# A conditioned transformer layer on one core: the front's stacks built and loaded by halves of the heads, the weight preparation moved, and one output projection placed among the score blocks

## What is computed

```python
c6 = jax.nn.silu(c) @ Wc + bc
sh_msa, sc_msa, g_msa, sh_mlp, sc_mlp, g_mlp = jnp.split(c6, 6, axis=-1)
xm = _modulate(_ln(x), sh_msa, sc_msa)
q, k, v = (xm @ Wq + bq), (xm @ Wk + bk), (xm @ Wv + bv)   # 16 heads of 16 features
w = softmax((q / DH) @ k^T)                                # 512 x 512 for each head
x = x + g_msa[:, None, :] * ((w @ v) @ Wo + bo)
xm2 = _modulate(_ln(x), sh_mlp, sc_mlp)
h = jax.nn.gelu(xm2 @ W1 + b1, approximate=False)          # 1024 wide
x = x + g_mlp[:, None, :] * (h @ W2 + b2)
```

## Time and profile before

| | us |
|---|---|
| median of three runs | 772.96 |
| the three runs | 769.92, 773.67, 772.96 |
| the profiled execution | 769.82 |
| its span in the profile | 768.0 |

### The profile page before, as it was taken

One profiled execution on the slowest core, in us unless ns is written; L12 is line 12 of the kernel. 1 busy time (PEld: TensorE's weight loads), 2 busy tenths in 40 slices (PEclk: granted clock), 3 DMA queues, 4 the chain that ended last, 5 costly groups with the idle time before them and its releaser, 6 DMA issues.

```text
span 768.0 us, 10579 instructions
## 1 busy us (share of the span) xinstructions
PE 709.2 (92%) x3967; PEld 383.4 (50%) x3967; DVE 580.4 (76%) x1019; ACT 391.3 (51%) x463; POOL 216.8 (28%) x162
## 2 busy tenths in 40 slices
PE   4698989869999999999999999999999998998986
PEld 2451222432368425762378326852477226812976
DVE  4779788859886998789887988789887976621463
ACT  5420556117752675358642875267633773398221
POOL 1454020200344032512253033413062122230444
PEclk8875799869999999999999999999999998999999
DMA  8599000771058302850067303930175102021110
GB/s 299 204 260 254 22 29 15 254 175 55 29 174 228 99 29 100 248 165 29 28 213 176 111 28 125 257 117 29 45 259 142 55 29 72 15 71 45 56 35 28
DMA packets 59839, 88.36 MB, mean 115 GB/s; under 512 B 6246, under 2 KB 47740, under 8 KB 56716
## 3 DMA queue, kind: packets, MB, share of 16 engines
q1 hardware_dynamic: 59788, 87.69, 37.4%
HBM read 49.35 MB, written 38.06 MB: 114 GB/s over the span
## 4 chain that ended last, share of the span: by engine, by line
PE 67%; DVE 16%; issue 6%; DMA 5%; ACT 4%; POOL 1%; SPq 0%; ACTq 0%; DVEq 0%
PE ps L646 15%; PE ps L624 14%; PE ps L654 12%; PE ps L569 10%; DVE mx L942 8%; PE ps L790 7%; PE ps L794 3%; ACT prob L515 2%; DVE prob L1014 2%; PE ps L606 2%; DMA qst<-mrow 2%; DVE prob L1017 1%; ACT z L493 1%; DMA xa<-in_x_dram 1%; PE ps L726 1%
## 5 line engine op out<-in xcount | busy, mean ns | idle before, releaser
L942 DVE TENSOR_REDUCE mx<-ps 128x1 f32<-128x512 f32 x512 | 335.8, 685 | 58.8 <-PE ps L624 53.8
L515 ACT ACTIVATE prob<-ps 128x1024 f32<-128x1024 f32 x256 | 247.8, 1022 | 152.7 <-PE ps L654 152.5
L624 PE MATMUL ps<-kst,qst 96*128 96x512 bf16 x512 | 198.4, 409 | 19.3 <-DVE mx L942 16.8
L654 PE MATMUL ps<-qst,kst 98*128 98x512 bf16 x512 | 150.1, 384 | 4.6 <-DMA qst<-mrow 2.6
L624 PEld LDWEIGHTS ps<-kst,qst 96*128 96x128 bf16 x512 | 45.7, 98 | 186.8 <-DVE mx L942 164.7
L646 PE MATMUL ps<-prob,vaug 128*32 128x512 f32 x1024 | 137.2, 608 | 0.3 <-ACT prob L515 0.3
L457 POOL TENSOR_TENSOR hl<-z,hh 128x512 fp32r<-128x512 f32 x64 | 82.3, 1287 | 138.1 <-DVE hh L1074 138.1
L556 ACT ACTIVATE z<-ps,bias_t 128x512 f32<-128x512 f32 x64 | 44.0, 688 | 134.5 <-PE ps L794 128.9
L404 POOL TENSOR_TENSOR rstd<-vare,mhalf 128x4 f32<-128x4 f32 x16 | 16.7, 1046 | 252.2 <-DVE vare L870 252.2
L654 PEld LDWEIGHTS ps<-qst,kst 98*128 98x128 bf16 x512 | 46.9, 99 | 70.7 <-ACT prob L515 27.2
L447 POOL TENSOR_TENSOR prob<-prob 128x512 bf16<-128x512 f32 x32 | 38.3, 1198 | 139.5 <-DVE prob L1017 139.5
(11 more groups left out here) (106 smaller groups left out, 833.5 us busy)
## 6 DMA issues: line engine op xcount, KB each, us to landing
parts_scratch<-prob SPq DMA_DIRECT2D x32, 384.0 KB, 3.0
qst<-parts_scratch SPq DMA_DIRECT2D x16, 768.0 KB, 9.4
kst<-parts_scratch SPq DMA_DIRECT2D x16, 768.0 KB, 14.4
parts_scratch<-prob SPq DMA_DIRECT2D x32, 256.0 KB, 3.2
y_scratch<-rb SPq DMA_DIRECT2D x32, 256.0 KB, 2.0
xa<-in_x_dram SPq DMA_DIRECT2D x8, 512.0 KB, 4.6
parts_scratch<-prob SPq DMA_DIRECT2D x32, 128.0 KB, 2.9
xd<-in_x_dram SPq DMA_DIRECT2D x8, 512.0 KB, 3.4
```

What stands on the lines that cost most here:

```text
L515: act.activation(prob[:, s % 2, 2 * p:2 * p + 2, :], ps[:, 2 * p:2 * p + 2, :], ACT.Exp, scale=1.0 / DH).then_inc(exp_done, 1)
L624: pe.matmul(ps[:, banks[n % len(banks)], :], qst[1 - par][0:MROW, h, t * P:(t + 1) * P], kst[1 - par][0:MROW, h, :], start=True, stop=True ...
L654: m = pe.matmul(ps[:, q, :], kst[par][0:KROWS, G * g + q, kt * P:(kt + 1) * P], qst[par][0:KROWS, G * g + q, :], start=True, stop=True)
L942: dve.tensor_reduce(mx[:, t, h:h + 1], ps[:, banks[n % len(banks)], :], AXX, ALU.max).then_inc(max_done, 1)
```

## The change

- **Front, input.** x of batch 1 goes into `x1` right after Wq and Wk are requested (before: into `xa`, after batch 0's normalised rows had been transposed). In step -2 its normalisation stands before the addition to the modulation rows on DVE.
- **Front, weights.** The split of Wv and Wo goes from DVE to ACT (high) and POOL (low). W1 and W2 are no longer loaded in the front but in step 0, in two times two transfers, into `x1` and `xn[1]`; their high parts are made on ACT after the exponentials of passes 3, 4, 11 and 12, their low parts on POOL, 1024 columns each. The constant rows of `kst[1]` go from POOL to ACT, half in step -2 and half in step -1.
- **Parts and stacks.** The order of the four blocks becomes q and k of the first half of the heads, then of the second (`ORDER`), in all steps. In the front a half is loaded as soon as it is written; elsewhere only the order of the four loads changes. `bo_b` and `b2_b` are loaded in the front after the stacks of batch 0.
- **Score blocks.** Eight blocks of batch 0 stand among the q, k and v products of batch 1 in step -1 (`EARLY_QK`, `EARLY_V`). Batch 1's last 24 blocks use four banks.
- **End of step 0.** `y_norm` stands before the last eight reductions, the Wo products stand among the last five score blocks, and `first_transposed` of batch 1 comes last.

```diff
+ORDER = (0, 2, 1, 3)
...
+EARLY_QK, EARLY_V = (0, 2, 0, 2), (1, 1, 1, 1)
...
+def max_banks(*stretches):
+    used, bank_of, back = {}, [], []
+    for n, banks in enumerate(banks for banks, blocks in stretches for _ in range(blocks)):
+        bank = min(banks, key=lambda b: used.get(b, -1))
+        bank_of.append(bank)
+        back.append(n - used[bank] if bank in used else 0)
+        used[bank] = n
+    return tuple(bank_of), tuple(back)
...
+MAX_FIRST = max_banks(((6, 7, 0, 1), HALF + 2), ((6, 7), NH * TT - HALF - 2))
+MAX_SECOND = max_banks(((6, 7), sum(NEW_BLOCKS)), ((6, 7, 0, 1), NH * TT - sum(NEW_BLOCKS)))
+MAX_STEADY = max_banks(((6, 7), NH * TT))
...
+AHEAD, BESIDE = 3, (2, 1, 1, 1)
...
+MLP_STEPS = (3, 4, 11, 12)
...
-        mlp_stage = kst[1][:].rearrange("p h s -> p (h s)").bitcast(F32)
...
+        mlp_stage = [a[:].rearrange("p t f -> p (t f)") for a in (x1, xn[1])]
+        w_mlp = [[a[:].rearrange("p c f -> p (c f)") for a in w] for w in (w1, w2)]
...
+            sp.dma_start(x1[:], x[1].rearrange("(t p) f -> p t f", p=P)).then_inc(xb_loaded, 16)
...
-            sp.dma_start(mlp_stage[:, 0:2048].rearrange("p (c f) -> p c f", c=KC), W1.rearrange("(c p) f -> p c f", p=P))\
-                .then_inc(wmlp_loaded, 16)
-            sp.dma_start(mlp_stage[:, 2048:4096].rearrange("p (c f) -> p c f", c=JT), W2.rearrange("(c p) f -> p c f", p=P))\
...
+            def mlp_weights(n):
+                for k in range(2):
+                    sp.dma_start(mlp_stage[k], (W1[k * P:(k + 1) * P, :], W2[k * 4 * P:(k + 1) * 4 * P, :].rearrange("(c p) f -> p c f", p=P))[n])                        .then_inc(wmlp_loaded[n], 16)
...
                 sp.dma_start(c6_scr[:], stage[0:NB, 1, 256:256 + 6 * H]).then_inc(c6_written, 16)
+                for d, b in ((bo_b, bo), (b2_b, b2)):
+                    sp.dma_start(d[:], b.rearrange("(o f) -> o f", o=1).broadcast_to([P, H])).then_inc(rows_loaded, 16)
...
+                if at(i, 0):
+                    sp.wait_ge(tp_done[0], 2)
+                    mlp_weights(0)
...
+                        if g == 0 and at(i, 0):
+                            sp.wait_ge(mlp_rest, 2)
+                            mlp_weights(1)
...
-                if early(i) and later(i, 2, 1):
+                if early(i):
                     for m in range(KC):
-                        sp.wait_ge(stack_loaded[m], 32)
-                if runs(i, 2):
+                        if later(i, 2, 1):
+                            sp.wait_ge(stack_loaded[m], 32)
+                        write_parts(i + 2, 2 * m)
+                        write_parts(i + 2, 2 * m + 1)
+                        if not later(i, 2, 1):
+                            sp.wait_ge(c6_done, 2)
+                        elif m == 0:
+                            sp.wait_ge(c6_written, 16)
+                            sp.wait_ge(mod_turned, 2)
+                            sp.wait_ge(bias_turned, 1)
+                            sp.wait_ge(w_split, 2)
+                            sp.wait_ge(vo_split, 2)
+                        load_stack(i + 2, 0, m)
+                        load_stack(i + 2, 1, m)
+                    if not later(i, 2, 1):
+                        modulation_rows()
+                elif runs(i, 2):
                     write_parts(i + 2, 0)
                     write_parts(i + 2, 1)
...
-                if runs(i, 2):
-                    if early(i) and later(i, 2, 1):
-                        sp.wait_ge(c6_written, 16)
-                        sp.wait_ge(mod_turned, 2)
-                        sp.wait_ge(bias_turned, 1)
-                        sp.wait_ge(w_split, 4)
-                    if early(i) and not later(i, 2, 1):
-                        modulation_rows()
-                        sp.wait_ge(c6_done, 2)
-                    load_stack(i + 2, 0, 0)
-                    load_stack(i + 2, 0, 1)
-                    if early(i) and later(i, 2, 1):
-                        sp.wait_ge(const_set, 5)
-                    load_stack(i + 2, 1, 0)
-                    load_stack(i + 2, 1, 1)
+                if runs(i, 2) and not early(i):
+                    for m in range(KC):
+                        load_stack(i + 2, 0, m)
+                        load_stack(i + 2, 1, m)
...
+            def value_weights():
+                w = slice(2, 4)
+                pool.wait_ge(vo_split, 1)
+                pool.tensor_tensor(wqkvo[1][:, w].rearrange("p n c f -> p (n c f)"), stage[:, 0, 1024:2048],
+                                   wqkvo[0][:, w].rearrange("p n c f -> p (n c f)").bitcast(F32), ALU.subtract).then_inc(vo_split, 1)
+            def mlp_weights(n):
+                for k in range(2):
+                    f = slice(1024 * k, 1024 * k + 1024)
+                    pool.wait_ge(mlp_split, 2 * n + k + 1)
+                    pool.tensor_tensor(w_mlp[n][1][:, f], mlp_stage[k], w_mlp[n][0][:, f].bitcast(F32), ALU.subtract).then_inc(mlp_rest, 1)
...
+                if at(i, 0):
+                    mlp_weights(0)
...
                     norm(0, 0)
+                    value_weights()
                     norm(0, 1)
...
+                    if at(i, 0):
+                        mlp_weights(1)
...
+            def constant_rows(n, first, last):
+                act.activation(kst[n][MROW:KROWS, first:last, :], mhalf[MROW:KROWS, 0:1].unsqueeze(2).broadcast_to([KROWS - MROW, last - first, S]),
+                               ACT.Copy, scale=2.0).then_inc(krows_set, 1)
+            constant_rows(0, 0, NH)
...
+                        if at(i, 0) and s in MLP_STEPS:
+                            n, k = divmod(MLP_STEPS.index(s), 2)
+                            act.wait_ge(wmlp_loaded[n], 32)
+                            act.activation(w_mlp[n][0][:, 1024 * k:1024 * k + 1024], mlp_stage[k], ACT.Copy).then_inc(mlp_split, 1)
...
+                if early(i) and not later(i, 2, 1):
+                    act.wait_ge(wqkvo_loaded[1], 32)
+                    act.activation(wqkvo[0][:, 2:4].rearrange("p n c f -> p (n c f)"), stage[:, 0, 1024:2048], ACT.Copy).then_inc(vo_split, 1)
...
+                    for n, j in enumerate(ORDER):
+                        act.wait_ge(qk_done, 4 * b + n + 1)
...
+                if early(i):
+                    constant_rows(1, 8 * (i + 2), 8 * (i + 2) + 8)
...
+                banks, back = max_of(i + 1)
...
-                    for w in range(2):
-                        for m in range(2):
-                            if w == 0 and has_c:
-                                pe.wait_ge(y_evac, NG * (i + 1) + m - 1)
+                    for m in range(2):
+                        for w in range(2):
...
+                                    pe.matmul(ps[:, QK_BANKS[2 * m + w], :], wqkvo[n][:, w, k, m * P:(m + 1) * P], zh[0][:, k, :],
...
+                            scores(i, par, qk_blocks(i)[2 * m + w])
...
+                        scores(i, par, v_blocks(i)[t])
...
-                    scores(i, par, HALF + 2, (6, 7, 0, 1))
+                    scores(i, par, HALF + 2 - block_at[0])
                     turn_maxima(i, 0, NH // 2, half_turned, 4)
                     scores(i, par, EXTRA - 2)
                 else:
-                    scores(i, par, tail_blocks(i))
+                    scores(i, par, tail_blocks(i) - sum(BESIDE))
+                    pe.wait_ge(vaug_done, 2 * (i + 3))
+                    for n, products in enumerate((wo_high, wo_low)):
+                        for t in range(TT):
+                            products(4, t)
+                            if t % 2:
+                                scores(i, par, BESIDE[2 * n + t // 2])
                     turn_maxima(i)
-                if has_c and not final(i):
-                    if has_mlp:
-                        pe.wait_ge(gelu_done, JT * i)
-                    elif has_a:
-                        pe.wait_ge(vaug_done, 2 * (i + 3))
+                    first_transposed(i + 1, 1 - par)
+                if has_mlp and has_c and not final(i):
+                    pe.wait_ge(gelu_done, JT * i)
                     wo_products(4)
...
-            def split_weights(turn):
-                w = slice(2 * turn, 2 * turn + 2)
-                src = stage[:, 0, 1024 * turn:1024 * turn + 1024]
-                dve.wait_ge(wqkvo_loaded[turn], 32)
+            def query_weights():
...
+                w = slice(0, 2)
+                src = stage[:, 0, 0:1024]
+                dve.wait_ge(wqkvo_loaded[0], 32)
...
-                        statistics(0, 1, xa, t)
+                        statistics(0, 1, x1, t)
                     variance(0, 1)
-                    split_weights(1)
...
-                for j in range(4):
-                    if j == 3:
-                        row_max(i, others(QK_BLOCKS[3] + sum(V_BLOCKS[0:2])))
+                    dve.wait_ge(rest_done, 4 * b + n + 1)
+                    dve.tensor_copy(parts[:, j, 1, :], rest[:, n % 2, :]).then_inc(part_m, 1)
+                for n in range(4):
```

(24 more changed lines are left out.)

160 lines of the change are left out of this document (83 added, 77 removed).

## The result

Twelve executions of the changed kernel have a median of 773.47 us (772.32 to 775.78), twelve of the kernel before 770.9 us (768.21 to 773.67). The ratio is 1.0036, its 95% interval 1.0018 to 1.0053: the change costs 1.4 to 4.1 us. The forecast was 1.8 us faster. The time lies inside the range of 767 to 774 and within 0.5% of before, but the sign was wrong.

What follows compares the result with a forecast made beforehand. PE bounds the full steps; the front is one chain, and PE and DVE bound the first attention. Front -4.6, hold +2.8, end of step 0 at 0: 772.96 - 1.8 = 771.2 us, range 767.0 to 774.0.

Steps and rivals of the forecast that it cites:

- GpSimd against VectorE: First attention, passes 11 to 13: POOL's subtractions hold two VectorE normalisation pieces 1.0 and 2.1 us; +2.8 us, bounds 0 to 3.1.
- rival 1: First attention: only the first normalisation piece is held, or POOL waits for DVE; net -3.8 us, 769.2 us; chance 0.18.
- Front: Everything up to the first attention: the 34th row maximum comes at 65.8 instead of 70.4 us, 4.6 earlier, range 3 to 6.
- z0 to z1: Front, ScalarE's z (modulated input) of batch 0 to batch 1's: the latter starts at 33.75 instead of 37.40 us, 3.65 earlier.
- z1 to the 34th maximum: Front, batch 1's z to its last row maximum: 32.05 us instead of 33.0, 0.95 less.
- Batch 1's stacks are done by about 65: Front's queue: batch 1's stacks finish before the maxima rows want the queue at 67; 2 us of room, cost nothing.
- Does batch 0's stack come in time?: Front: first half lands by 38, wanted at 40.3; second by 46, wanted at about 64; cost nothing.
- Rival 3: Front doesn't deliver: ACT's constant rows or the stack land 2 to 4 us late; net +0.2, 773.2 us; chance 0.10.
- End of step 0: New order after the first attention: maxima rows requested 5 us later but hidden behind stack loads; 0, range -0.5 to +1.
- rival 4: End of step 0: `rb` lands at 158, not 152.5, stalling DVE and PE; net +2.9, 775.9 us; chance 0.08.
- ScalarE's casts: First attention: each 1024-column cast fits a 1.12 us gap between exponentials; cost nothing, at most 0.8 us in all.
- Full steps at nothing: Full steps (168 to 284 us): PE almost always busy, only parts and stack-load order changed; no effect counted.

Runs made afterwards that it cites:

- the first pair of profiles: First profiled executions of the changed kernel and the kernel before, without further edits: 775.78 us for the changed one, 6.0 us above before; spans 774.0 and 768.0.
- the second profile of before: The kernel before, unchanged, profiled once more: 768.64 us, span 766.8.

## Why the prediction went wrong

Two terms of the sum failed, and by the first pair of profiles or the second either would have turned the sign alone: the hold, where 2.7 us for PE's lower clock were left out, and the front, which gave 3.3 or 2.3 us less than was put down for it.

- **GpSimd against VectorE: right mechanism, term mis-sized, +2.8 against +5.5.** The step forecast which pieces are held, until when, and one at 1.4 and one at 2.5 us; they took 1.15 and 2.52, and the holds of 2.87 us are what the term had. The failing step is "of the 3.1 us the bank traffic absorbs 0.2 to 0.5; I take +2.8": it let PE stand for 2 us and charged only those. The prediction reckons with PE's lower clock at the end of step 0, but here its price was left out of the sum and of the bounds (0 to 3.1); 2.7 us of it came on top of the holds. The Trainium skill's page "SBUF — State Buffer", section "Who interferes with whom", gives the lock and the exemption of tensor_reduce; the trace agrees with both (1.15 and 2.52 us beside a subtraction, four reductions in 2.59 with or without one). What decided the second hold is not so clear. The prediction had the piece 0.2 us too late, and hung rival 1 on that; by the profile it began at 120.39, 0.03 us ahead of the subtraction (120.42), and was held all the same, as in the four other profiles with both held. The recorded starts on GpSimd are rough, so they can't say which came first.
- **Front, -4.6 against -1.3 and -2.3: mis-sized.** Three parts. (1) z0 to z1 was forecast as 20.26 us (33.75 less 13.49) and took 20.86 and 21.05. That is right to 0.8 us, but the whole chain hung from the z0 of one profile, 13.49, the earliest of fourteen, which spread up to 15.71 (1.1 us of it by the start of the Wc product, 1.1 by the slow transposes), and the second profile of before had a z0 to z1 of 23.02 and not 23.91. A saving read off one execution was too large by about 1 us for that alone. (2) z1 to the 34th maximum: 32.05 forecast, 31.99 to the end of the reductions measured (31.92 to the cast of the table). Right. But before itself took 32.93 or 32.20, so the gain is 1.0 or 0.3. (3) "Batch 1's stacks are done by about 65, before the maxima rows want the queue at 67 ... nothing" was wrong. The step put the second half of batch 0 at 34 and 36; it was requested at 41.55 and 43.45. By the timeline the writes that it reads back were issued behind the first half's loads (30.93), and in batch 1 the same again: VectorE's last part was ready at 51.83, its write was issued from 56.08, behind a load at 55.66, and the readback at 64.36 and 66.47. The late queue costs 0.4 to 0.5 us in the changed kernel itself (6.14 and 6.00 against 5.61) and 4.2 where the maxima rows are 3.8 us earlier: a ceiling. In the six profiles in which PE waited for the rows with the half stacks ahead of them, it began 7.0 to 8.4 us after the last half stack's request, however early the rows were. With the half stacks ahead of the rows no profile of eight had its exponentials before 72.3; with them behind, four had them from 68.5 to 72.4.
- **Does batch 0's stack come in time?** Right: the first half was requested at 29.26 and 30.57 (27 and 29 forecast), and PE did not wait for it. Rival 3 came near the time (773.2) by a mechanism that did not happen: luck.
- **End of step 0, 0 (range -0.5 to +1) against +1.1 to +1.3.** At the edge of its range. `rb` was requested where before had it (152.78 less the 4.37 us that z2 had slipped is 148.41) but landed at 155.1 in that count, not 152.5. Half of rival 4 came true: 4.02 us idle before the division, where over 3 was named as its sign. The experiments leave open whether the new end of step 0 makes this term.
- **ScalarE's casts.** Right: 1.06 us each, the next exponentials 0 to 0.21 us late. **Full steps at nothing.** Right: 555.2 to 557.8 us in all profiles.
- **The sum.** -1.8 forecast; to it 2.7 for the clock, 3.3 or 2.3 for the front, 1.1 to 1.3 for the end of step 0, and 1.8 or 0.6 in the first part of step 1 (42.9 and 44.1 before, 44.7 after, and 44.4 to 45.1 in all variants) make 7.1 in the first pair and 5.1 in the second; the other columns add -1.1 and +1.1, which gives the 6.0 and 6.2 between the profiles. The medians differ by 2.6 and 4.9. No term stood for the first part of step 1. Its length goes with PE's lower clock in all fourteen profiles: 42.9 us with none, 44.1 and 44.4 with 3.3 to 3.4 us of it, 44.5 to 45.1 with 4.3 to 7.1. That the clock is the cause was not tried.
- **The range.** That the time lies inside it is luck. Both terms left their own bounds (5.5 against at most 3.1, 1.3 and 2.3 against at least 3), and the median of before came out at 770.9 where the range was built on 772.96; on that, the loss of 2.6 us would have been 775.5.

## What to carry to other kernels

A wait that stops PE can be charged twice, for its own length and for the products at the lower clock behind it: two holds of 2.87 us together cost 5.5 here, one of 0.75 us cost 0.75. When a step lets PE stand for 2 us, its upper bound has to hold the second charge. A sum should not start from one profile either: the first z alone spread over 2.2 us. Place such GpSimd subtractions beside reductions and not beside normalisations: one table of four numbers was worth 5 us here. And before a front is made faster, follow the small transfer that ends it through its queue: large readbacks that nobody needs yet, requested ahead of it, give back whatever the compute gained.
